# Macaron block: V projected in rounded passes and turned on VectorE, the mask written by ScalarE, new orders on every engine

## What is computed

```
x = attn_layer(shift_tokens(x), Wqkv[i], q_scale[i], k_scale[i], Wo[i]) + x
x = ffn_layer(shift_tokens(x), ln_g[i], ln_b[i], W1[i], b1[i], W2[i], b2[i]) + x

q, k, v = jnp.split(x @ Wqkv, 3, -1)          # 16 heads of 64
q, k = l2norm(q) * qs, l2norm(k) * ksc        # then rotary tables with a scale
sim = jnp.einsum('bhwie,bhwje->bhwij', bq, bk2) * 8.0   # windows of 32, keys of 2 windows
sim = jnp.where(mask, -jnp.finfo(sim.dtype).max, sim)
out = jnp.einsum('bhwij,bhwje->bhwie', softmax(sim), bv2) @ Wo
```

## Time and profile before

| | |
|---|---|
| median of 3 runs | 3544.3 us (3540.96 to 3550.66) |
| the profiled execution's own time | 3533.41 us |
| its span | 3531.6 us |
| mean granted TensorE clock | 0.957 |
| TensorE matmul busy | 3063.9 us, 87% |
| VectorE busy | 2855.9 us, 81% |
| GpSimd busy | 2377.3 us, 67% |
| ScalarE busy | 2034.7 us, 58% |

### The profile page before, as it was taken

The page is one execution under the profiler, slowest core; times in us unless marked ns, Lnnn a source line. Parts: engine busy times, 40 slices in busy tenths (PEclk is TensorE's granted clock), DMA queues, the critical chain, the costliest instruction groups (busy, mean ns, idle before and its releaser), DMA issues. The chain is left out here.

```text
span 3531.6 us, 140825 instructions
## 1 busy us (share of the span) xinstructions
PE 3063.9 (87%) x62504; PEld 1720.0 (49%) x62504; DVE 2855.9 (81%) x3936; ACT 2034.7 (58%) x3781; POOL 2377.3 (67%) x1599
## 2 busy tenths in 40 slices
PE   5789989988989989987666798989899989989986
PEld 2445555555555545553332455555555555555553
DVE  5778888888888788876896788888888888888884
ACT  2466566565566565555663466556556556566563
POOL 3677777777767777674453677767767777767772
PEclk7899999999999999998897899999999999999997
DMA  4333333332332333320002333332333333333320
GB/s 124 69 80 71 86 83 70 82 86 67 81 80 68 81 84 69 80 62 25 9 6 51 72 80 70 79 85 66 76 86 70 80 84 71 80 86 68 81 67 13
DMA packets 126727, 250.03 MB, mean 71 GB/s; under 512 B 27436, under 2 KB 71080, under 8 KB 126120
## 3 DMA queue, kind: packets, MB, share of 16 engines
q1 hardware_dynamic: 126120, 241.03, 28.8%
HBM read 36.45 MB, written 3.15 MB: 11 GB/s over the span
## 5 line engine op out<-in xcount | busy, mean ns | idle before, releaser
L1231 POOL TENSOR_TENSOR q_ring<-q_ring,partner 128x512 f32<-128x512 f32 x384 | 509.6, 1327 | 550.0 <-DMA partner<-sines 549.8
L1064 ACT ACTIVATE squares<-general 128x512 f32<-128x512 f32 x768 | 456.2, 595 | 724.5 <-PE general L653 707.6
L876 DVE SCALAR_TENSOR_TENSOR sines<-general,vec,consts 128x512 f32<-128x512 f32 x768 | 566.4, 737 | 332.1 <-ACT squares L1064 300.4
L1251 POOL TENSOR_TENSOR probs<-probs,row_sum 128x1024 f32<-128x1024 f32 x192 | 365.9, 1906 | 385.4 <-DVE row_sum L953 384.5
L1231 POOL TENSOR_TENSOR k_ring<-k_ring,partner 128x512 f32<-128x512 f32 x384 | 507.6, 1322 | 0.0
L663 PE MATMUL general<-att,wo 128*128 128x512 f32 x768 | 389.7, 642 | 78.1 <-ACT att L1130 70.0
L744 PE MATMUL general<-wv,xs 128*32 128x256 f32 x6144 | 433.0, 395 | 24.5 <-issue 24.4
L687 PE MATMUL general<-probs_t,v_buf 32*64 32x64 f32 x24576 | 332.7, 232 | 134.6 <-issue 60.6
L687 PEld LDWEIGHTS general<-probs_t,v_buf 32*64 32x64 f32 x24576 | 299.3, 132 | 274.4 <-issue 266.4
L651 PE MATMUL general<-xs_hi,wqk_lo 128*128 128x512 f32 x768 | 389.1, 507 | 10.9 <-DVE xs_lo L894 7.5
L1245 POOL TENSOR_TENSOR probs<-probs,q_scale 128x1024 f32<-128x1024 f32 x192 | 368.0, 1917 | 15.1
(11 more groups left out here) (229 smaller groups left out, 5628.1 us busy)
## 6 DMA issues: line engine op xcount, KB each, us to landing
partner<-sines SPq DMA_DIRECT2D x1536, 128.0 KB
wqk_raw<-in_wqkv SPq DMA_DIRECT2D x80, 128.0 KB, 2.4
wv<-in_wqkv SPq DMA_DIRECT2D x12, 512.0 KB, 4.0
wo<-in_wo SPq DMA_DIRECT2D x12, 512.0 KB, 5.1
w<-in_w SPq DMA_DIRECT2D x12, 341.0 KB, 3.6
base_dram<-x SPq DMA_DIRECT2D x8, 256.0 KB, 2.4
att<-in_wqkv SPq DMA_DIRECT2D x4, 512.0 KB, 4.8
sines<-base_dram SPq DMA_DIRECT2D x8, 256.0 KB, 3.9
```

What stands on the lines that cost most here:

```text
L876: e.scalar_tensor_tensor(out=by_seq(sines[:, i % 2, which, :]), in0=g, scalar=scale, in1=both(tables[:, 2 * which + 1, :]), op0=ALU.mult, ...
L1064: e.activation(squares[:, (2 * p + which) % 4, :], general_of(("proj", k, n, p, which))[:, :], ACT.Square).then_inc(S[f"squared_{side}"], 1)
L1231: e.tensor_tensor(y, y, partner[:, which, :], ALU.add).then_inc(S[f"rotated_{side}"], 1)
L1251: e.tensor_tensor(y, y, spread_keys(row_sum[:, i % 2, :]), ALU.mult).then_inc(S["probs_done"], 1)
```

## The change

**V by columns.** The weights of V are laid out anew on the host and lie behind Q and K of each pair, 416 columns in all, so that they are loaded, rounded and split with them. `pe_v` has the weights as 128x128 weights and streams 256 tokens, in the same three rounded passes as Q and K, once for each sequence, which is six matmuls for a pair. V is made one step behind its pair instead of four. What lies in PSUM then is V by columns, and VectorE turns it in blocks of 32x32 into `v_buf` (`dve_v`). The copy on ScalarE is gone, and the separate load of V weights too. Heads are placed by (q + seq) % 4 instead of q ^ seq.

**The mask.** Where the score bank was last written in full by matmuls, ScalarE copies the mask into it ahead of its step (`act_mask`), and the scores are added over that; else the matmul stays. `Banks` finds 366 of the 384 banks to be such.

**Low parts.** GpSimd subtracts for the low part of the 80 weight pairs that are loaded within a stack (`pool_split_pair`); the 16 first ones stay on VectorE. The high and low parts of the inverse key norms lie in different rows of one tile (`inv_parts`), so that the selecting matmul needs one pass instead of two.

**Smaller ones.** The variance and the sums of squares are turned straight from PSUM, and the constant is added to the few turned columns that are used. ScalarE, not VectorE, evicts the centred tokens. The output projection has two parts of four pairs instead of three (two, two, four), at lags 17 and 21 instead of 14, 16 and 21, so one addition less. The last shift of the last four items of a stack is left out, as nothing reads it.

**Orders.** All four lists of a step are written in a new order, and the order of the banks follows.

```
-V_LAG = 4
+V_LAG = 1
...
-OUT_PAIRS = ((0, 1), (2, 3), (4, 5, 6, 7))
+OUT_PAIRS = ((0, 1, 2, 3), (4, 5, 6, 7))
...
-        self.out_first = next(((self.item(t, at), i) for i, at in ((0, 14), (1, 16)) if self.item(t, at) is not None), None)
+        self.out_first = next(((self.item(t, at), i) for i, at in ((0, 17),) if self.item(t, at) is not None), None)
...
-                    pe_bank(w, ("scores", k, n, group, seq))
-                    e.matmul(g[seq][:, :], ident_bf[:, :], mask_bf[:, :], start=True, stop=False, skip_group_check=True)
+                    key = ("scores", k, n, group, seq)
+                    if BANKS.filled[key]:
+                        w.wait_ge(S["mask_set"], MASKED[key])
+                    else:
+                        pe_bank(w, key)
+                        e.matmul(g[seq][:, :], ident_bf[:, :], mask_bf[:, :], start=True, stop=False, skip_group_check=True)
...
-                e.matmul(g[:, cut], sel, inv_lo[:, cut], start=True, stop=False)
-                done = e.matmul(g[:, cut], sel, inv_hi[:, cut], start=False, stop=True)
+                done = e.matmul(g[:, cut], sel, inv_parts[:, cut], start=seq == 0, stop=True, skip_group_check=True)
...
-            for j in range(2):
-                win = 2 * p + j
-                seq = win // NWIN
-                lhs = xs[:, c * CHUNK_SEQS + seq, (win % NWIN) * WIN:(win % NWIN + 1) * WIN]
-                for q in range(4):
-                    rhs = wv[:, layer % 2, :].rearrange("d (r g c) -> d g r c", g=4, c=DH)[:, q ^ seq, :, :]
-                    done = e.matmul(g[32 * q:32 * q + 32, j * 256:(j + 1) * 256], lhs, rhs, start=True, stop=True)
+            for seq in range(CHUNK_SEQS):
+                cut, cols = slice(seq * SEQ, (seq + 1) * SEQ), slice(W_V + seq * WIN, W_V + seq * WIN + P)
+                e.matmul(g[:, cut], wqkv_lo[:, p, cols], xs_hi[:, r, cut], start=seq == 0, stop=False, skip_group_check=True)
+                e.matmul(g[:, cut], wqkv_hi[:, p, cols], xs_lo[:, r, cut], start=False, stop=False, skip_group_check=True)
+                done = e.matmul(g[:, cut], wqkv_hi[:, p, cols], xs_hi[:, r, cut], start=False, stop=True, skip_group_check=True)
...
+        def dve_v(e, w, k, n, p):
+            m, half = k * ITEMS + n, p % 2
+            w.wait_ge(S["v_projected"], m * PAIRS + p + 1)
...
+            at = p // 2 * DH + half * WIN
+            e.transpose(v_buf[:, n % 2, :, at:at + WIN], general_of(("v", k, n, p)).rearrange("p (w c) -> p w c", c=WIN))\
+                .then_inc(S["v_kept"], 1)
...
+        def act_mask(e, w, k, n, group):
+
+            for seq in range(CHUNK_SEQS):
+                key = ("scores", k, n, group, seq)
+                if BANKS.filled[key]:
+                    w.wait_ge(S["bf16_consts"], 1)
+                    w.wait_ge(S[BANKS.free(key)[0]], BANKS.free(key)[1])
+                    e.activation(general_of(key)[:, :], mask_bf[:, :], ACT.Copy).then_inc(S["mask_set"], 1)
...
+        def pool_split_pair(e, w, k, layer, p):
+            w.wait_ge(S["wqkv_hi"], (k * DEPTH + layer) * PAIRS + p + 1)
+            for cut, part in raw_of(p):
+                e.tensor_tensor(wqkv_lo[:, p, cut], part, wqkv_hi[:, p, cut].bitcast(F32), ALU.subtract).then_inc(S["wqkv_lo"], 1)
```

More of the change, by code:

```diff
@@ L228, in __init__ @@
     def __init__(self):
-        self.of, self.before, self.last = {}, {}, {}
+        self.of, self.before, self.last, self.written, self.filled = {}, {}, {}, {}, {}
         self.around(2)
@@ L240, in around @@
     def around(self, banks):
-        self.banks, self.next = banks, 0
+        self.banks, self.next, self.written = banks, 0, {}
     def use(self, key, sem, value):
@@ L245, in use @@
         self.next = (at + 1) % self.banks
-        self.of[key], self.before[key] = at, self.last.get(at)
+        self.of[key], self.before[key], self.filled[key] = at, self.last.get(at), self.written.get(at, False)
         self.last[at] = (sem, value)
+        self.written[at] = key[0] in ("proj", "v", "spread", "scores", "project", "ffn_out", "center", "var")\
+            or key[0] in ("gate", "value") and HIDDEN_CUTS[key[3]][1] == P
     def index(self, key):
@@ L264, in stack @@
             self.var(("enter", k, 0))
[L265 removed]
+        for st in PLAN:
             g = k * ITEMS
[L267 to L270 removed]
+            if st.now:
+                n, p = st.now
+                self.use(("proj", k, n, p, 0), "cos_q", (g + n) * PAIRS + p + 1)
             if st.spread:
@@ L299, in stack @@
                     self.use(("att", k, n, group, j), "att_kept", ((g + n) * GROUPS + group) * 4 + j + 1)
-            if st.gates is not None:
-                for j in range(len(HIDDEN_CUTS)):
-                    self.use(("gate", k, st.gates, j), "gelu_done", (g + st.gates) * 3 + j + 1)
             if st.v:
@@ L305, in stack @@
                 self.use(("v", k, n, p), "v_kept", (g + n) * PAIRS + p + 1)
-            if st.out_first:
-                n, i = st.out_first
-                self.use(("project", k, n, i), "att_added", (g + n) * 3 + i + 1)
-            for what in BESIDE[k]["PE"].get(t, ()):
+            for what in BESIDE[k]["PE"].get(st.t, ()):
                 self.part(what)
@@ L494, in macaron_kernel @@
                 for key in (("att", k, st.out_last), ("ffn", k, st.ffn_out), ("enter", k, st.enter[0] if st.enter and st.enter[1] == 2 else None)):
-                    if key[2] is not None:
+                    if key[2] is not None and key[2] not in (range(ITEMS - CHUNKS, ITEMS) if key[0] == "ffn" else ()):
                         count += 1
@@ L805, in tensor_stack @@
                     pe_v(e, w, k, *st.v)
-                if st.out_first:
-                    pe_out(e, w, k, *st.out_first)
-                for what in BESIDE[k]["PE"].get(t, ()):
+                for what in BESIDE[k]["PE"].get(st.t, ()):
                     tensor_part(e, w, *what)
@@ L1041, in scalar_program, with act_center, wait_xn_read @@
             scalar_stack(e, w, 1)
+        def act_center(e, w, key):
+            i = LN_ORDER[key]
+            w.wait_ge(S["ln_centered"], i + 1)
+            w.wait_ge(S["ln_scaled"], i)
+            wait_xn_read(w, i)
+            e.activation(centered[:, :], general_of(("center", key))[:, :], ACT.Copy).then_inc(S["ln_kept"], 1)
+        def wait_xn_read(w, i):
+            before = next((key for key, at in LN_ORDER.items() if at == i - 1), None)
+            if before and before[0] == "ffn":
+                w.wait_ge(S["value_done"], (before[1] * ITEMS + before[2]) * 3 + 3)
+            elif before and before in LN_AFFINE:
+                w.wait_ge(S["ln_affine"], LN_AFFINE[before])
         def act_root(e, w, key):
```

433 lines of the change are left out of this document (221 added, 212 removed).

## The result

The changed kernel takes **3518.56 us** in the median of five runs (3517.63 to 3525.06), the kernel before 3540.96 beside it (3533.58 to 3550.66): a ratio of **0.9938**, 95% interval 0.9918 to 0.9958. The forecast was 3465. So 22 us are gained where I had worked out 79. One execution of the last run of all (3518.6 us) was in a slower state of the chip, and its ratio is that of the other three.

What follows compares the result with a forecast made beforehand. GpSimd's rotations and the partner DMA bound the kernel, 62.4 of 64.4 us an item. Saving 69 us in 46 items and 5 in the tail takes 3533 to 3459; the median's 11 more gives 3465, range 3380 to 3570.

Steps and rivals of the forecast that it cites:

- this ring: GpSimd's rotations and the partner DMA, waiting for each other through one `partner`, set the pace: 7.8 us a step; chance 54%.
- My 62.4 us: Estimated item time of the cycle of GpSimd's rotations (2.5 us a step) and partner transfer (5.3), against 64.4 measured.
- my signs of being right: Period near 62.9 us, DMA holding back three rotations in four or more, inverse waits below 2.0, V's slot near 0.75.
- I take 1.5 of the 2.0: 46 x 1.5 = 69: GpSimd's waits beyond the DMA's landing: earlier inverse and no weights' wait save 1.5 of 2.0 us an item, 69 us.
- The weights' wait: VectorE's wait for ScalarE's rounded weights before splitting them, 1.75 us an item, gone with the split.
- The 5 us for the tail: At the program's end a shift of 1.3 us drops out at some places, starts alike: 5 us less.
- TensorE's work: TensorE's busy time per item falls from 58.7 to 54.5 us through cheaper mask, spread and V.
- TensorE's idle above 5.7 an item: Sign of being right: TensorE's idle time per item rises above 5.7 us, as it is cheaper but not faster.
- TensorE alone (3351): Rival: TensorE sets the pace, so all 4.2 us an item go through, 193 us, giving 3351; chance 17%.
- The third rival: ScalarE's three GELUs delay VectorE's norms and K in p = 1, 2.1 us; 3650 if nothing covers it; chance 14%.
- Nothing comes of it: Rival: VectorE keeps its waits apart from the weights', 64.6 us an item, time 3545; chance 10%.
- VectorE's sum: VectorE's busy time per item: 5.7 us more for V's turns, 3.7 less elsewhere, so 53.8 to 55.8.

Runs made afterwards that it cites:

- Relieving the ring: The kernel before with only the partner transfer split into two halves, Q's and K's DMAs waiting separately: ratio 0.9936.
- only together with less work on TensorE: The kernel before with the partner transfer in two halves and one of Q's three projection products left out: ratio 0.9816.
- the same edit: The changed kernel with the partner transfer split into two halves, Q's and K's DMAs waiting separately: ratio 0.9802, 3461 us.
- 1.8 us less: One of the three products of Q's projection left out, in two runs: ratio 1.0002 in the kernel before, 0.9934 in the changed kernel.
- the mask, 2.1 us in the scores' steps: The changed kernel with the mask written by TensorE again for all scores' banks: ratio 1.0079.
- 43.5 us less work on it: The changed kernel with VectorE turning only half of each V block, the other half left at zero: ratio 0.9952.

## Why the prediction was wrong, and where it was right

**"I take this ring to set the pace": wrong for the kernel before.** I had taken "the DMA held back the rotation in three steps of four" and SyncE's 0.1 us behind the rotation as proof. They show a chain with no slack inside it, but so do other chains when everything runs at one pace. Relieving the ring left the item at 65.0 us there; only together with less work on TensorE did it pay. For the changed kernel, in which TensorE has been relieved, the ring is a part of the bound: the same edit is worth 1.4%, 1.1 us an item, where my theory of it had asked for 3 to 8. My 62.4 us came close to the item because the longer transfers and waits in it had been measured inside that item; that they fitted proved nothing. Nor did my signs of being right: the period near 62.9 us (63.2 in the stretch I looked at), the DMA still holding the rotation back (123 times), shorter waits for the inverse (0.9 us each) and V's slot near 0.75 us (0.81) all came true, and the gain did not.

**"I take 1.5 of the 2.0: 46 x 1.5 = 69": the term that failed.** The inverse came earlier, as forecast (its wait fell from 120.6 to 27.5 us), and its order was worth nothing: 0.9947 with it turned back, against 0.9938. GpSimd spent 60 of these 93 us waiting for the DMA instead. I had taken the wait for the inverse as time on the path without asking what would be waited for next. The weights' wait, the other half of the term, was not tried alone. The forecast also had every item gain alike, and the second interval of each stack lost 19 us together. The 5 us for the tail are nearly right by themselves, as the program ends 98 us after the last item's norms are turned back instead of 106, but the first such turn comes 7 us later than before.

**TensorE's work: right, its price wrong.** 54.7 us busy against 54.5; V's six passes 0.81 us against 0.75 (0.69 in the median from the first start to the last, and 0.12 for the last); V's turn on VectorE 686 ns against 0.71; GpSimd 1.5 more against 1.7. I had "TensorE's idle above 5.7 an item" as harmless, and it is 8.5. What I left out is the clock: its mean fell from 0.99 to 0.97, and 181 instead of 68 us of those 2340 were spent at 1.2 GHz. The useless matmuls, which hold the clock, gave back 29 us of the 54 that the forecast was off by; whether by the clock alone is open, as said above.

The Trainium skill (TensorE: Matmul & The Clock Gate, Part 1) says that throttled is the array's default and activity releases it, and that this is no boost. The traces agree: useless work in two idle places took the time at the lower level from 181 to 82 us.

**The rivals.** TensorE alone (3351) falls, as 4 us per item less busy time gained 22 us of 193, and 1.8 us less changed nothing in either kernel; but the mask, 2.1 us in the scores' steps, was worth 50 us, so neither it nor the ring alone is the story. The third rival named the right step and its waits, and 0.9945 says that its order cost nothing by itself. "Nothing comes of it" (3545) was nearest to the size, for another reason: VectorE did not keep its waits, and with 43.5 us less work on it nothing changed.

**VectorE's sum: 56.9 busy against 55.8.** The shrunken pass over the norms I had at 0.25 us, and low parts at the price of before:

```profile
L913 DVE TENSOR_SCALAR norm_t<-norm_t x48: 226/796/1356, 87.2 to 3418.8; 128x128 f32<-128x128 f32 x48
```

```profile
L929 DVE SCALAR_TENSOR_TENSOR inv_parts<-inv_hi,consts,inv_norm x48: 743/1517/2500, 93.0 to 3431.6; 128x512 fp32r<-128x512 f32 x48
L897 DVE TENSOR_TENSOR xs_lo<-xs,xs_hi x48: 672/1216/2410, 25.3 to 3338.6; 128x512 fp32r<-128x512 f32 x48
```

The clamp takes 227 ns when no GpSimd instruction runs beside it (4 of 48) and 841 in the median when one does nearly throughout (42 of 48, from 226 to 1356). Before, it read PSUM, four times as many columns, and took 649, with GpSimd beside it or not. Shrinking it to a quarter and moving it to SBUF made it dearer. The run without the clamp shows that this cost no time here.

The Trainium skill (SBUF — State Buffer, who interferes with whom) has the exclusive lock for a VectorE operation in a two-port mode too, not only for one with two SBUF inputs; I had applied it to the split alone. The 227 and 841 ns agree with it, and so do the 649 from PSUM.

## What to carry to other kernels

A wait that follows its releaser without slack does not name the bound. Add up an engine's waits by all their releasers before counting one of them as time to be gained: what is taken from one can turn up at the next. Take the item's time from the whole run and not from its middle, since a gain there can be lost at the start. With two cycles of nearly one length, relieving either shows nothing, so try edits in pairs before giving one up. Time saved on TensorE that turns into idle time may be partly paid back at the lower clock; look at the granted clock of the stretch before counting it as gained.

## What was not expected of the hardware

Useless matmuls at two places of an item made the kernel 29 us faster, and leaving out real ones beside them made it 20 us slower (0.9855 to 0.9912).

The partner transfer has a floor: from the end of a rotation to the next, 4.25 to 4.28 us at the least in each of the eight steps, in the kernel before and in the changed one; the means of the steps lie above it by up to 1.8 us before. In the changed kernel the records of instruction loads (q8, 457 packets) overlap 185 of the 190 such gaps over 5 us, and 40 of the 129 under 4.5. A longer gap has more room for a packet, and whether they lengthen it was not tried.

```profile
q8 instruction: 457, 7.49, 0.9%
```
